# Graph attention on one core: the second attention's tiles written out in line, with a general pass behind them

## Chip, cores and metric

The kernel runs on one core of a Trainium2 chip. The metric is the device time of one execution in microseconds, the median of three runs. Within the core five engines work in parallel, each on its own instruction queue: TensorE (PE; its weight loads are PEld), VectorE (DVE), ScalarE (ACT), GpSimd (POOL) and SyncE (SP). They meet only at semaphores.

## What is computed

The reference is a stack of four layers over 6250 nodes of 256 numbers and 100,000 edges, sorted by destination: a cheap attention, a mixture of 6 experts, the graph attention that is changed here, and a mixture of 8 experts. Everything is float32. The third layer, cut to what matters (h is the normalised x times W, in 4 heads of 64):

```python
src = concatenate([edge_src, arange(n)]); dst = concatenate([edge_dst, arange(n)])
e = a_src[src] + a_dst[dst]              # 4 scores per edge
e = where(e > 0, e, 0.2 * e)
m = segment_max(e, dst)
ex = exp(e - m[dst])
denom = segment_sum(ex, dst)
alpha = ex / (denom[dst] + 1e-16)
out = segment_sum(alpha[:, :, None] * h[src], dst)
x = x + relu(out + bias)
```

How many edges end in a stretch of 128 nodes depends on the data: about 2048 (100,000 over 6250, times 128), a little more or less from tile to tile.

## The kernel before

The function `gnn_moe` runs the stages one after the other: `setup`, `project` and `experts` for the first layers, `project` "b0", `attention`, and again `project`, `experts` and `finish`.

**Tables.** Nodes are cut into 49 tiles of 128. During the first `project`, the class `EdgeRanges` finds for each tile the run of granules (32 edges each) that touches it. A *step* handles 17 chunks of 128 edges, 2176 edges or 68 granules (`SE`, `SEG`). The table `K.ET` holds for each tile its first edge, its number of steps n, and the number s0 of its first step. A tile whose run is longer than 68 granules has n = 2.

**One step of `attention`.** SP loads the source list `idx` and the destination list `dcol`, in three groups of 6, 6 and 5 chunks. POOL issues one indirect DMA for each chunk, which gathers 128 rows of 260 numbers (h and its score) into `G`. DVE compares the destinations with the ids of the tile (`one_hots`, into `OH`); PE transposes these one-hots (`turn`), ACT keeps them (`keep_turned`, into `OT`), and PE looks up the destination's part of the score (`destinations`, into `pAd`). DVE makes the scores (`scores`, four short instructions on `Z`), ACT takes the exponential (`exps`), DVE multiplies the gathered rows by it (`weigh`), and PE sums them by destination (`aggregate`, 17 matmuls that the trace shows as two records each, into `pAgg`). DVE adds that to `ACC` (`absorb`), and after a tile's last step divides, adds the bias and updates x (`finalize`).

**Loops.** Every engine runs loops over tiles, and within them over steps, with the number of steps read at run time from `K.ET`; POOL and ACT loop over all steps at once. What sets the order is each engine's written program and the semaphores. `G` has one buffer for each group of chunks, so a group's gathers of the next step wait until `aggregate` has read the last ones (`agg_done[j]`); other groups go on meanwhile, so the steps overlap.

Of the kernel before, what the change touches and what calls it, by code (L numbers as in the profile page):

```python
# [12 lines left out]
P = 128  # L13
# [30 lines left out]
GRAN = 32  # L44
# [47 lines left out]
def gnn_moe(nc, out, x, src, dst, L0_gnn_weight, L0_gnn_attn_l, L0_gnn_attn_r, L0_ffn_router_w1, L0_ffn_router_b1, L0_ffn_router_w2, L0_ffn_router_b2, L0_ffn_expert_w1, L0_ffn_expert_b1, L0_ffn_expert_w2, L0_ffn_expert_b2, L0_ffn_expert_w3, L0_ffn_expert_b3, L1_gnn_W, L1_gnn_att_src, L1_gnn_att_dst, L1_gnn_bias, L1_ffn_Wg, L1_ffn_bg, L1_ffn_W1, L1_ffn_b1, L1_ffn_W2, L1_ffn_b2):  # L92
    with ExitStack() as whole:
# [71 lines left out]
        K.ET = sb("edge_steps", [1, TILES, 3], I32)  # L165
        K.AD = sb("as_ad", [P, TILES, 8])
# [108 lines left out]
class EdgeRanges:  # L275
# [4 lines left out]
    def __init__(self, K, sb, sem):  # L280
# [9 lines left out]
        self.row = sb("row", [1, TILES, 2])  # L290
# [15 lines left out]
    def turn(self, gp):  # L306

        K = self.K
        gp.wait_ge(self.step, 13)
        gp.dma_start(K.RT[:, :], self.span[:, :]).then_inc(self.span_out, 16)  # L310
        gp.wait_ge(self.span_out, 16)
        gp.dma_start(self.row[0:1, :, :], K.RT.rearrange("(o t) k -> o t k", o=1)).then_inc(self.row_in, 16)
        gp.wait_ge(self.row_in, 16)
# [28 lines left out]
    def table(self, v):  # L342
# [8 lines left out]
        ch.mark(nc.vector.tensor_tensor(K.ET[0:1, :, 2], inc[0:1, :], row[0:1, :, 1], ALU.subtract))  # L351

# [966 lines left out]
def attention(K, bias_in):  # L1319
# [6 lines left out]
    J = range(len(CHUNKS))  # L1326
    with ExitStack() as stack:
# [4 lines left out]
        exs = sb("exs", [P, TILES, HEADS])  # L1332
        pm = sem("pm")
        gm_ready = sem("gm_ready")
        gm_all = sem("gm_all")
        self_z = sem("self_z")
        with nc.Block() as block:
            @block.vector
            def _(v):
                V = nc.vector  # L1340
                ch = Chain(v, pm)
                AS, ADs = K.AD[:, :, 0:4], K.AD[:, :, 4:8]
                ch.mark(V.tensor_reduce(gm[:, :].rearrange("p (h o) -> p h o", o=1),
                                        K.AD[:, 0:TILES - 1, 0:4].rearrange("p t h -> p h t"), AX.X, ALU.max))
                ch.link(V.tensor_scalar(gt[:, :], K.AD[:, TILES - 1, 0:4], K.vneg[:, 0:1], None, ALU.add))
                V.tensor_tensor(gm[:, :], gm[:, :], gt[:, :], ALU.max).then_inc(gm_ready, 1)
                v.wait_ge(gm_all, 1)
# [13 lines left out]
            @block.scalar  # L1361
            def _(act):
                act.wait_ge(self_z, 1)
                nc.scalar.activation(exs[:, :, :], exs[:, :, :], ACT.Exp)

        idx = [sb(f"idx{j}", [P, CHUNKS[j]], I32) for j in J]
        dcol = [sb(f"dcol{j}", [P, CHUNKS[j]]) for j in J]
        G = [sb(f"G{j}", [P, CHUNKS[j], DIM + 4]) for j in J]
        OH = [sb(f"OH{j}", [P, CHUNKS[j], P]) for j in J]
        OT = [sb(f"OT{j}", [P, CHUNKS[j], P]) for j in J]  # L1370
        Z = [sb(f"Z{j}", [P, CHUNKS[j], HEADS]) for j in J]
        own = sb("own", [P, DIM + 4])
        cur = sb("cur", [P, 8])
        ACC = sb("ACC", [P, DIM + 4])
        bias = sb("bias", [P, DIM])
        res = sb("res", [P, DIM])
        rec = sb("rec", [P, HEADS])
        pAd = [pb(f"pAd{j}", [P, 512]) for j in J]
        pAgg = pb("pAgg", [P, 512])


        pIds = pb("pIds", [P, 512])
        TI = pIds[:, 0:P]
        pEx = [pIds[:, P + j * 64:P + (j + 1) * 64] for j in J]
        pTr = [pb(f"pTr{h}", [P, 512]) for h in range(2)]

        bias_ld = sem("bias_ld")
        init = sem("init")
        src_in = [sem(f"src_in{j}") for j in J]
        dst_in = [sem(f"dst_in{j}") for j in J]  # L1390
        gathered = [sem(f"gathered{j}", software=True) for j in J]
        onehots = [sem(f"onehots{j}") for j in J]
        agg_done = [sem(f"agg_done{j}") for j in J]
        own_in = sem("own_in")
        own_used = sem("own_used")
        cur_ready = sem("cur_ready")
        ad_ready = sem("ad_ready")
        scored = [sem(f"scored{j}") for j in J]
        ex_ready = sem("ex_ready")
        msg_ready = sem("msg_ready")  # L1400
        acc_done = sem("acc_done")
        turned = sem("turned")
        ot_ready = sem("ot_ready")
        chain = sem("chain")
        passed = sem("passed")
        NJ = len(CHUNKS)
        lifts = (own_used, acc_done, ot_ready, *scored, *onehots, *agg_done)
        START, STEP, END = 2, 3 * NJ, 5

        def tile_steps(eng, t):  # L1410
            at = slice(t, t + 1) if isinstance(t, int) else bass.ds(t, 1)
            n = eng.value_load(K.ET[0:1, at, 1:2].rearrange("o a b -> o (a b)"), min_val=1, max_val=MAXSTEPS)
            s0 = eng.value_load(K.ET[0:1, at, 2:3].rearrange("o a b -> o (a b)"), min_val=0, max_val=TILES * MAXSTEPS)
            return n, s0

        with nc.Block() as block:
            @block.sync
            def _(sp):
                sp.dma_start(bias[:, :], bias_in.partition_broadcast(P)).then_inc(bias_ld, 16)
                with sp.Fori(0, TILES) as t:  # L1420
                    n, s0 = tile_steps(sp, t)
                    base = sp.value_load(K.ET[0:1, bass.ds(t, 1), 0:1].rearrange("o a b -> o (a b)"), min_val=0, max_val=EDGES - GRAN)
                    r0 = sp.snap(t * P)
                    freed(sp, own_used, t)
                    sp.dma_start(own[:, :], K.T1[bass.ds(r0, P), :]).then_inc(own_in, 16)
                    with sp.Fori(0, n) as g:
                        s = sp.snap(s0 + g)
                        e0 = nc.s_assert_within(sp.snap(base + g * SE), 0, EDGES, skip_runtime_bounds_check_because=
                                                "a step begins before its tile's last edge, and SE edges of padding follow the last")
                        at = [sp.snap(e0 + OFFS[j]) for j in J]  # L1430
                        for j in J:
                            ne = CHUNKS[j] * P
                            freed(sp, scored[j], s)
                            sp.dma_start(idx[j][:, :], K.SRCP[bass.ds(at[j], ne)].rearrange("(p c) -> p c", p=P)).then_inc(src_in[j], 16)
                            freed(sp, onehots[j], s)
                            sp.dma_start(dcol[j][:, :], K.DSTP[bass.ds(at[j], ne)].rearrange("(p c) -> p c", p=P)).then_inc(dst_in[j], 16)
# [3 lines left out]
            def _(gp):  # L1440
                lift(gp, lifts)
                n, s0 = tile_steps(gp, TILES - 1)
                with gp.Fori(0, gp.snap(s0 + n)) as s:
                    for j in J:
                        gp.wait_ge(src_in[j], s * 16 + 16)
                        freed(gp, agg_done[j], s)
                        gp.sem_inc(passed, 1)
                        for c in range(CHUNKS[j]):
                            gp.indirect_dma_start(G[j][:, c, :], None, K.T1,  # L1449
                                                  bass.IndirectOffsetOnAxis(ap=idx[j][:, c:c + 1], axis=0)).then_inc(gathered[j], 16)  # L1450

            @block.vector
            def _(v):
                V = nc.vector

                def one_hots(s, j):
                    c = CHUNKS[j]
                    v.wait_ge(dst_in[j], s * 16 + 16)
                    freed(v, agg_done[j], s)
                    V.tensor_tensor(OH[j][:, :, :], dcol[j][:, :].rearrange("p (c o) -> p c o", o=1).to_broadcast([P, c, P]),  # L1460
                                    TI.rearrange("p (o n) -> p o n", o=1).to_broadcast([P, c, P]),
                                    ALU.is_equal).then_inc(onehots[j], 1)

                def scores(ch, s, j):
                    c = CHUNKS[j]
                    v.wait_ge(gathered[j], s * (16 * c) + 16 * c)
                    v.wait_ge(ad_ready, s * NJ + j + 1)
# [224 lines left out]
```

## Time and profile before

| | |
|---|---|
| median of 3 runs | 3005.16 us (3003.9 to 3005.75) |
| the profiled execution's own time | 3002.53 us |
| span in its trace | 3000.9 us |
| second attention's gathers, first to last start | 921.20 to 1986.75 us |
| last update of x by the second attention | ends at 1998.46 us |
| mean granted TensorE clock | 0.822 |

The span is the time from the first to the last instruction of the profiled execution; 1.6 us of its own time lie outside it. Times within the trace count from the start of the span. Each row of a timeline has start, duration, engine, line and operation, output and inputs, and in square brackets how long the engine was idle before and what ended that.

### The profile page before, as it was taken

How to read it: one execution, taken by the hardware profiler on the slowest of the kernel's cores; microseconds unless marked ns; L12 is line 12 of the kernel's file. 1: busy time of each engine (PE TensorE's matmuls, PEld its weight loads, DVE VectorE, ACT ScalarE, POOL GpSimd, SP SyncE). 2: the span in 40 equal slices, each digit the busy share in tenths (PEclk: the TensorE clock that was granted, in tenths of full speed). 3: DMA queues.
4: the chain of work that ended last, by engine and by line, in shares of the span. 5: the costliest groups of instructions: out<-in, count | busy, mean ns of one | idle time of the engine just before them, and what ended most of it. 6: DMA issues, size and time to landing. Idle time of an engine off the chain costs nothing. (4 is left out here: it accounts for less than half of the span.)

```text
span 3000.9 us, 51618 instructions
## 1 busy us (share of the span) xinstructions
PE 2097.8 (70%) x12494; PEld 1844.3 (61%) x12495; DVE 1610.3 (54%) x4211; ACT 826.5 (28%) x2262; POOL 1437.8 (48%) x1457
## 2 busy tenths in 40 slices
PE   2533229898475787888878877866078998898970
PEld 2433227777354666666666666656078898888970
DVE  6365613222473556555555565556166655766555
ACT  1333302222141111111111111123044554545530
POOL 1267633333105777777777777736523322323220
PEclk8756569999796888888888888865589999999985
DMA  6212242222353444444444444422412221312207
GB/s 147 83 49 77 78 119 93 92 94 91 106 169 92 114 112 113 113 114 112 114 113 113 113 113 112 115 58 93 118 59 65 72 72 35 101 35 72 72 28 257
DMA packets 245332, 292.27 MB, mean 97 GB/s; under 512 B 102061, under 2 KB 199492, under 8 KB 245180
## 3 DMA queue, kind: packets, MB, share of 16 engines
q0 software_dynamic: 66224, 181.07, 20.9%
q1 hardware_dynamic: 165526, 97.08, 12.0%
q10 hardware_dynamic: 13544, 13.73, 1.4%
q14 instruction: 29, 0.24, 0.0%
q8 instruction: 9, 0.15, 0.0%
HBM read 213.94 MB, written 78.22 MB: 97 GB/s over the span
## 5 line engine op out<-in xcount | busy, mean ns | idle before, releaser
L1449 POOL DMA_INDIRECT at_G<-h_as,at_idx x850 | 806.7, 949 | 269.2 <-issue 256.4
L1600 PE MATMUL at_pAgg<-at_G,at_OH 128*128 128x260 f32 x1700 | 542.1, 484 | 158.6 <-DVE at_ACC L1498 95.7
L1600 PEld LDWEIGHTS at_pAgg<-at_G,at_OH 128*128 128x128 f32 x1700 | 404.5, 245 | 260.4 <-DVE at_G L1480 179.2
L1063 POOL DMA_INDIRECT expert_out<-e_ob,e_to x212 | 205.1, 968 | 743.5 <-DVE e_ob L1294 711.2
L1480 DVE TENSOR_TENSOR at_G<-at_G,at_pIds 128x1536 f32<-128x1536 f32 x150 | 249.8, 1665 | 151.4 <-ACT at_pIds L1565 151.4
L1267 DVE TENSOR_TENSOR e_hT_low<-e_full,e_hT_high 128x256 fp32r<-128x256 f32 x432 | 226.4, 531 | 156.9 <-ACT e_hT_high L1214 155.9
L1137 PE MATMUL e_pH<-e_xT_high,e_WA_high 128*128 128x256 f32 x864 | 257.2, 298 | 75.3 <-DVE e_xT_low L1229 68.1
L1558 ACT ACTIVATE at_OT<-at_pTr 128x384 f32<-128x384 f32 (+1 forms) x300 | 125.8, 470 | 656.8 <-PE at_pTr L1585 656.5
L1213 ACT ACTIVATE e_full<-e_pH,e_BA 128x256 f32<-128x256 f32 x432 | 219.0, 507 | 206.8 <-PE e_pH L1139 136.8
L1138 PE MATMUL e_pH<-e_xT_low,e_WA_high 128*128 128x256 f32 x864 | 249.3, 289 | 0.0
L1139 PE MATMUL e_pH<-e_xT_high,e_WA_low 128*128 128x256 f32 x864 | 249.1, 288 | 0.0
L1137 PE MATMUL e_pO<-e_WL_high,e_hT_high 128*128 128x256 f32 x864 | 245.1, 284 | 0.5 <-DVE e_ob L1294 0.5
L1138 PE MATMUL e_pO<-e_WL_low,e_hT_high 128*128 128x256 f32 x864 | 240.7, 279 | 0.0
L1139 PE MATMUL e_pO<-e_WL_high,e_hT_low 128*128 128x256 f32 x864 | 240.4, 278 | 0.0
L1593 PEld LDWEIGHTS at_pAd<-at_cur,at_OT 128*128 128x128 f32 x1700 | 208.7, 201 | 43.6 <-ACT at_OT L1558 43.6
L1593 PE MATMUL at_pAd<-at_cur,at_OT 128*128 128x8 f32 x1700 | 212.4, 261 | 31.7 <-ACT at_OT L1558 31.7
L1137 PEld LDWEIGHTS e_pH<-e_xT_high,e_WA_high 128*128 128x128 f32 x864 | 172.7, 200 | 83.6 <-issue 72.0
L1214 ACT ACTIVATE e_hT_high<-e_pH,e_BA 128x256 fp32r<-128x256 f32 x432 | 220.7, 511 | 0.0
L1138 PEld LDWEIGHTS e_pH<-e_xT_low,e_WA_high 128*128 128x128 f32 x864 | 172.5, 200 | 0.0
L1139 PEld LDWEIGHTS e_pH<-e_xT_high,e_WA_low 128*128 128x128 f32 x864 | 171.5, 199 | 0.0
L1137 PEld LDWEIGHTS e_pO<-e_WL_high,e_hT_high 128*128 128x128 f32 x864 | 162.4, 188 | 0.7 <-DVE e_ob L1294 0.7
L1138 PEld LDWEIGHTS e_pO<-e_WL_low,e_hT_high 128*128 128x128 f32 x864 | 162.3, 188 | 0.0
(294 smaller groups left out, 3680.2 us busy)
## 6 DMA issues: line engine op xcount, KB each, us to landing
e_xs<-slot_rows SPq DMA_DIRECT2D x106, 257.0 KB
at_G<-h_as,at_idx POOLq DMA_INDIRECT x850, 2.8
b_rows<-expert_out SPq DMA_DIRECT2D x14, 896.0 KB
f_rows<-expert_out ACTq DMA_DIRECT2D x14, 896.0 KB, 7.7
e_rawA<-in_L_ffn_W_dram SPq DMA_DIRECT2D x8, 1024.0 KB, 5.0
e_rawL<-in_L_ffn_W_dram SPq DMA_DIRECT2D x8, 1024.0 KB
xt_ar<-a_og SPq DMA_DIRECT2D x7, 910.0 KB, 4.5
h_as<-b_og SPq DMA_DIRECT2D x7, 910.0 KB, 4.2
```

The lines of the kernel that those rows point to most:

```text
L1063: gp.indirect_dma_start(K.YS, bass.IndirectOffsetOnAxis(ap=to[b][:, s:s + 1], axis=0), ob[b][:, s, :], None).then_inc(sent[b], 16)
L1137: nc.tensor.matmul(out, left[0], right[0], start=start, stop=False)
L1138: nc.tensor.matmul(out, left[0], right[1], start=False, stop=False)
L1139: return nc.tensor.matmul(out, left[1], right[0], start=False, stop=stop)
L1213: nc.scalar.activation(full[u % 4][:, :], pH[u % 4][:, 0:MT], func, bias=at)
L1214: nc.scalar.activation(dst[b][0][:, c, :], pH[u % 4][:, 0:MT], func, bias=at).then_inc(h_ready, 1)
L1267: V.tensor_tensor(hT[b][1][:, u, :], full[u % 4][:, :], hT[b][0][:, u, :], ALU.subtract).then_inc(l_ready, 1)
L1449: gp.indirect_dma_start(G[j][:, c, :], None, K.T1, bass.IndirectOffsetOnAxis(ap=idx[j][:, c:c + 1], axis=0)).then_inc(gathered[j], 16)
L1480: V.tensor_tensor(rows, rows, ex, ALU.mult).then_inc(msg_ready, 1)
L1558: nc.scalar.activation(OT[j][:, a:z, :].rearrange("n c p -> n (c p)"), pTr[h][:, 0:(z - a) * P], ACT.Copy).then_inc(ot_ready, 1)
L1593: last = nc.tensor.matmul(pAd[j][:, 8 * c:8 * c + 8], OT[j][:, c, :], cur[:, :], start=True, stop=True)
L1600: last = nc.tensor.matmul(pAgg[:, 0:DIM + 4], OH[j][:, c, :], G[j][:, c, :], start=(j == 0 and c == 0), stop=(j == NJ - 1 and c == CHUNKS[ ...
```

## The change

There are now two passes in `attention`.

The **first pass** has no loops: SP, POOL, DVE, ACT and PE have the 49 tiles written out, one step for each. SP loads each tile's lists in one piece each, one tile ahead. `idx`, `dcol`, `own`, `OH`, `pAd` and `pAgg` have two buffers; `G`, `OT` and `Z` still have one for each group. DVE subtracts the tile's first id from the destinations (`localize`) and makes the one-hots of tile t + 1 before and between the scores of tile t. PE transposes them there too, and does all of a tile's lookups at its beginning. `finalize(t - 1)` starts the sum from the node's own row and takes `pAgg` in.

The **general pass** stands behind it and has loops over tiles and steps. In it, everything has one buffer. SP starts a step's loads when the step before is in `ACC` (`absorbed`), and DVE and POOL wait for all three of them (`loaded`); ACT begins the exponentials when all three groups are scored, DVE the weighing when all three exponentials are there, and PE the sums when all three groups are weighed.

Two new values in the tables join them. `K.FAST` is 1 when no tile has more than one step, else 0; `K.GEN` is 49 - 49 * `K.FAST` and is the number of tiles that the general pass runs over. The first pass always runs; its quotient and its bias are multiplied by `K.FAST`, so that with 0 it adds nothing to x. The row of step counts is for that loaded into all 128 partitions.

```diff
+        K.FAST = sb("one_step_each", [P, 1])
+        K.GEN = sb("general_tiles", [1, 1], I32)
...
+        ch.link(nc.vector.tensor_reduce(self.most[:, :], row[:, :, 1], AX.X, ALU.max))
+        ch.link(nc.vector.tensor_scalar(K.FAST[:, :], self.most[:, :], 1.5, None, ALU.is_lt))
+        ch.mark(nc.vector.tensor_scalar(K.GEN[:, :], K.FAST[0:1, :], -float(TILES), float(TILES), ALU.mult, ALU.add))
...
+                ch.mark(V.tensor_scalar(bias[:, :], GB[:, :], K.FAST[:, 0:1], None, ALU.mult))
...
+                for t in range(TILES):
+                    b, n = t % 2, 16 * (t // 2 + 1)
+                    e0 = sp.value_load(K.ET[0:1, t:t + 1, 0:1].rearrange("o a b -> o (a b)"), min_val=0, max_val=EDGES - GRAN)
+                    after(sp, scored, NJ * (t - 1))
+                    sp.dma_start(idx[b][:, :], K.SRCP[bass.ds(e0, SE)].rearrange("(p c) -> p c", p=P)).then_inc(idx_in[b], 16)
+                    after(sp, localized, t - 1)
+                    sp.dma_start(dcol[b][:, :], K.DSTP[bass.ds(e0, SE)].rearrange("(p c) -> p c", p=P)).then_inc(dst_in[b], 16)
+                    after(sp, own_used, t - 1)
+                    sp.dma_start(own[b][:, :], K.T1[t * P:(t + 1) * P, :]).then_inc(own_in[b], 16)
...
+                for t in range(TILES):
+                    b = t % 2
+                    gp.wait_ge(idx_in[b], 16 * (t // 2 + 1))
                     for j in J:
-                        gp.wait_ge(src_in[j], s * 16 + 16)
-                        freed(gp, agg_done[j], s)
-                        gp.sem_inc(passed, 1)
+                        after(gp, agg_done, NJ * (t - 1) + j + 1)
...
+                def finalize(t):
+
+                    b = t % 2
+                    v.wait_ge(own_in[b], 16 * (t // 2 + 1))
+                    V.tensor_tensor(ACC[:, 0:DIM].rearrange("p (h k) -> p h k", h=HEADS),
+                                    own[b][:, 0:DIM].rearrange("p (h k) -> p h k", h=HEADS),
+                                    exp_self[:, t, :].rearrange("p (h o) -> p h o", o=1).to_broadcast([P, HEADS, CH]), ALU.mult).then_inc(own_used, 1)
+                    ch.link(V.tensor_copy(ACC[:, DIM:DIM + 4], exp_self[:, t, :]))
+                    v.wait_ge(own_used, t + 1)
+                    v.wait_ge(agg_done, NJ * (t + 1))
+                    V.tensor_tensor(ACC[:, :], ACC[:, :], pAgg[b][:, 0:DIM + 4], ALU.add).then_inc(acc_read, 1)
+                    v.wait_ge(acc_read, t + 1)
...
+                    ch.link(V.tensor_scalar(rec[:, :], rec[:, :], K.FAST[:, 0:1], None, ALU.mult))
...
+                localize(0)
+                for j in J:
+                    one_hots(0, j)
+                for t in range(TILES):
+                    more = t + 1 < TILES
+                    if more:
+                        localize(t + 1)
+                        one_hots(t + 1, 0)
+                        one_hots(t + 1, 1)
+                    scores(t, 0)
+                    weigh(t, 0)
+                    if t:
+                        finalize(t - 1)
+                    if more:
+                        one_hots(t + 1, 2)
+                    scores(t, 1)
+                    weigh(t, 1)
+                    scores(t, 2)
+                    weigh(t, 2)
+                finalize(TILES - 1)
...
+                for j in J:
+                    turn(0, j)
+                for t in range(TILES):
+                    for j in J:
+                        destinations(t, j)
+                    for j in J:
+                        if t + 1 < TILES:
+                            turn(t + 1, j)
+                        aggregate(t, j)
...
+                m = general_tiles(sp)
+                with sp.If(m > 0):
+                    with sp.Fori(0, m) as t:
+                        n, s0 = general_steps(sp, t)
+                        first = sp.value_load(K.ET[0:1, bass.ds(t, 1), 0:1].rearrange("o a b -> o (a b)"), min_val=0, max_val=EDGES - GRAN)
+                        r0 = sp.snap(t * P)
+                        with sp.Fori(0, n) as g:
+                            s = sp.snap(s0 + g)
+                            e0 = nc.s_assert_within(sp.snap(first + g * SE), 0, EDGES, skip_runtime_bounds_check_because=
+                                                    "a step begins before its tile's last edge, and SE edges of padding follow the last")
+                            freed(sp, absorbed, s)
+                            sp.dma_start(idx[0][:, :], K.SRCP[bass.ds(e0, SE)].rearrange("(p c) -> p c", p=P)).then_inc(loaded, 16)
+                            sp.dma_start(dcol[0][:, :], K.DSTP[bass.ds(e0, SE)].rearrange("(p c) -> p c", p=P)).then_inc(loaded, 16)
+                            sp.dma_start(own[0][:, :], K.T1[bass.ds(r0, P), :]).then_inc(loaded, 16)
...
+                            gp.wait_ge(loaded, s * 48 + 48)
+                            gp.sem_inc(passed, 1)
+                            for j in J:
+                                for c in range(CHUNKS[j]):
+                                    gp.indirect_dma_start(G[j][:, c, :], None, K.T1,
+                                                          bass.IndirectOffsetOnAxis(ap=idx[0][:, FIRST[j] + c:FIRST[j] + c + 1], axis=0)).then_inc(got[j], 16)
...
+                    for j in J:
+                        c = CHUNKS[j]
+                        v.wait_ge(got[j], s * (16 * c) + 16 * c)
+                        v.wait_ge(looked_up, s + 1)
+                        ad = pAd[0][:, 8 * FIRST[j]:8 * (FIRST[j] + c)].rearrange("p (c k) -> p c k", k=8)
+                        ch.link(V.tensor_tensor(Z[j][:, :, :], G[j][:, :, DIM:DIM + 4], ad[:, :, 0:4], ALU.add))
+                        ch.link(V.scalar_tensor_tensor(Z[j][:, :, :], Z[j][:, :, :], 0.2, Z[j][:, :, :], ALU.mult, ALU.max))
+                        ch.link(V.tensor_tensor(Z[j][:, :, :], Z[j][:, :, :], ad[:, :, 4:8], ALU.subtract))
+                        V.tensor_scalar(Z[j][:, :, :], Z[j][:, :, :], 0.0, None, ALU.min).then_inc(rated, 1)
+                    for j in J:
+                        c = CHUNKS[j]
+                        v.wait_ge(weights_made, s * NJ + NJ)
+                        rows = G[j][:, :, 0:DIM].rearrange("p c (h k) -> p c h k", h=HEADS)
+                        ex = pEx[j].rearrange("p (c h o) -> p c h o", h=HEADS, o=1).to_broadcast([P, c, HEADS, CH])
+                        V.tensor_tensor(rows, rows, ex, ALU.mult).then_inc(weighed, 1)
+                    v.wait_ge(summed, s + 1)
+                    ch.mark(V.tensor_tensor(ACC[:, :], ACC[:, :], pAgg[0][:, 0:DIM + 4], ALU.add))
+                    ch.settle()
+                    v.sem_inc(absorbed, 1)
+
...
+                            for j in J:
+                                act.wait_ge(rated, s * NJ + NJ)
+                                nc.scalar.activation(G[j][:, :, DIM:DIM + 4], Z[j][:, :, :], ACT.Exp)
+                                nc.scalar.activation(pEx[j].rearrange("p (c h) -> p c h", h=HEADS), Z[j][:, :, :],
+                                                     ACT.Exp).then_inc(weights_made, 1)
...
+                            pe.wait_ge(weighed, s * NJ + NJ)
+                            for j in J:
+                                for c in range(CHUNKS[j]):
+                                    last = nc.tensor.matmul(pAgg[0][:, 0:DIM + 4], OH[0][j][:, c, :], G[j][:, c, :],
+                                                            start=(j == 0 and c == 0), stop=(j == NJ - 1 and c == CHUNKS[j] - 1))
+                            last.then_inc(summed, 1)
```

On SP, the issue order changes as follows. These rows are the loop body of before: `g_edge_steps` is the table read into registers, and three pairs of small loads make a step.

```order
L1425 DMA at_own<-h_as 128x260
L1426 UNCONDITIONAL_BRANCH
L1426 ISA
L1434 ISA
L1434 DMA at_idx<-src_padded 128x6
L1436 DMA at_dcol<-dst_padded 128x6
L1434 ISA
L1434 DMA at_idx<-src_padded 128x6
L1436 DMA at_dcol<-dst_padded 128x6
L1434 ISA
L1434 DMA at_idx<-src_padded 128x5
L1436 DMA at_dcol<-dst_padded 128x5
```

And this is the general pass's loop on SP in the changed kernel, from the last of its three table loads on:

```order
L1629 TENSOR_LOAD g_edge_steps
L1629 ISA x2
L1631 UNCONDITIONAL_BRANCH
L1631 ISA
L1636 ISA
L1636 DMA at_idx<-src_padded 128x17
L1637 DMA at_dcol<-dst_padded 128x17
L1638 ISA
L1638 DMA at_own<-h_as 128x260
L1631 REGISTER_ALU
L1631 COMPARE_AND_BRANCH
```

Three loads take the place of seven, the node's own rows last, and the whole list of a step comes in one piece. The first pass, ahead of it, has the same three kinds of load written out 49 times.

On DVE, before, the last group of a tile's step and the start of a further step of the same tile; `at_pIds` holds the tile's ids and the exponentials:

```order
L1480 TENSOR_TENSOR at_G<-at_G,at_pIds 128x5x256
L1531 COMPARE_AND_BRANCH
L1532 UNCONDITIONAL_BRANCH
L1532 ISA
L70 REGISTER_ALU
L1460 TENSOR_TENSOR at_OH<-at_dcol,at_pIds 128x768 x2
```

And in the general pass of the changed kernel, from the last group's last score to the update of `ACC` and on into the division:

```order
L1679 TENSOR_SCALAR at_Z<-at_Z 128x20
L1682 ISA
L1685 TENSOR_TENSOR at_G<-at_G,at_pExs 128x6x256 x2
L1685 TENSOR_TENSOR at_G<-at_G,at_pExs 128x5x256
L1687 TENSOR_TENSOR at_ACC<-at_ACC,at_pAgg 128x260
L85 REGISTER_ALU
L1707 REGISTER_ALU
L1707 COMPARE_AND_BRANCH
L1713 TENSOR_SCALAR at_rec<-at_ACC 128x4
```

The three multiplications stand together behind the last score, and the update of `ACC` stands directly behind them, where before other groups' and steps' work lay between.

## Rows read from the trace of the kernel before

**Rows 1.** The page's first line: span and instructions.

```profile
span 3000.9 us, 51618 instructions
```

**Rows 2.** Groups, 921 to 1997 us: count, busy us, mean ns, idle before.

```profile
L1449 POOL DMA_INDIRECT at_G<-h_as,at_idx x850 | 806.7, 949 | 269.2 <-issue 256.4 <-DMA at_idx<-src_padded 12.2 <-PE at_pAgg L1600 0.6
...
L1498 DVE TENSOR_TENSOR at_ACC<-at_ACC,at_pAgg 128x260 f32<-128x260 f32 x50 | 20.9, 418 | 3.1 <-PE at_pAgg L1600 3.1
...
L1524 DVE TENSOR_TENSOR at_ACC<-at_own,at_exs 128x256 f32<-128x256 f32 x49 | 20.4, 417 | 0.0
...
L1515 DVE TENSOR_SCALAR at_pIds<-at_pIds 128x128 f32<-128x128 f32 x48 | 14.4, 299 | 29.7 <-issue 29.7
```

**Rows 3.** Windows view: busy us of each engine, granted clock, DMA.

```profile
core 0: us, PE busy (x) PEld busy (x) DVE busy (x) ACT busy (x) POOL busy (x), PEclk, DMA share, GB/s
921.00:1997.00 1076.00, 863.15 (x4250) 711.52 (x4250) 620.17 (x1386) 165.63 (x600) 806.73 (x850) 0.83 0.43 112
```

**Rows 4.** Timeline of DVE, 1630 to 1662 us.

```profile
1630.40 0.30 DVE L1515 TENSOR_SCALAR at_pIds<-at_pIds 128x128 f32<-128x128 f32 x1 [0.63 <-issue]
...
1651.19 1.81 DVE L1460 TENSOR_TENSOR at_OH<-at_dcol,at_pIds 128x768 f32<-128x768 f32 x2
```

**Rows 5.** Timeline: DVE frees the own rows, SP's next load follows.

```profile
1513.42 0.42 DVE L1524 TENSOR_TENSOR at_ACC<-at_own,at_exs 128x256 f32<-128x256 f32 x1
...
1514.02 0.33 SPq L1425 DMA_DIRECT2D at_own<-h_as  x1
```

**Rows 6.** Timeline: the attention's first loads and gather.

```profile
914.94 0.36 SPq L1419 DMA_DIRECT2D at_bias<-in_L_gnn_bias_dram  x1
...
917.64 0.36 SPq L1425 DMA_DIRECT2D at_own<-h_as  x1
918.41 0.34 SPq L1434 DMA_DIRECT2D at_idx<-src_padded  x1
918.84 0.38 SPq L1436 DMA_DIRECT2D at_dcol<-dst_padded  x1
...
920.55 1.85 DVE L1460 TENSOR_TENSOR at_OH<-at_dcol,at_pIds 128x768 f32<-128x768 f32 x2 [0.98 <-DMA at_dcol<-dst_padded]
...
921.20 1.19 POOL L1449 DMA_INDIRECT at_G<-h_as,at_idx  x1 [9.48 <-DMA at_idx<-src_padded]
```

**Rows 7.** DMA issues, 921 to 1997 us: KB each, us to landing.

```profile
at_own<-h_as SPq DMA_DIRECT2D x48, 130.0 KB, 2.1
```

**Rows 8.** Timeline: the attention's last group, to its last update.

```profile
1986.75 0.95 POOL L1449 DMA_INDIRECT at_G<-h_as,at_idx  x1 [0.30 <-issue]
...
1990.45 0.17 DVE L1469 TENSOR_TENSOR at_Z<-at_G,at_pAd 128x20 f32<-128x20 f32 x1 [0.79 <-DMA at_G<-h_as,at_idx]
...
1991.29 0.22 ACT L1564 ACTIVATE at_G<-at_Z 128x20 f32<-128x20 f32 x1 [3.41 <-DVE at_Z L1473]
...
1991.62 1.49 DVE L1480 TENSOR_TENSOR at_G<-at_G,at_pIds 128x1280 f32<-128x1280 f32 x1 [0.36 <-ACT at_pIds L1565]
1996.24 0.42 DVE L1498 TENSOR_TENSOR at_ACC<-at_ACC,at_pAgg 128x260 f32<-128x260 f32 x1 [3.14 <-PE at_pAgg L1600]
...
1998.04 0.42 DVE L1509 SCALAR_TENSOR_TENSOR g_x<-at_res,g_x 128x256 f32<-128x256 f32 x1
```

**Rows 9.** Timeline of PE: sums of two groups, and lookups.

```profile
933.57 5.00 PE L1600 MATMUL at_pAgg<-at_G,at_OH 128*128 128x260 f32 x12 [3.99 <-DVE at_G L1480]
...
989.68 2.46 PE L1600 MATMUL at_pAgg<-at_G,at_OH 128*128 128x260 f32 x10 [0.28 <-DVE at_G L1480]
...
994.32 2.74 PE L1593 MATMUL at_pAd<-at_cur,at_OT 128*128 128x8 f32 x24
```

**Rows 10.** Windows view of PE: length, busy us, granted clock, DMA.

```profile
935.50:937.50 2.00, 2.00 (x6) 0.50 0.66 178
937.50:939.00 1.50, 1.50 (x9) 0.88 0.32 89
...
945.50:948.00 2.50, 1.58 (x8) 1.00 0.46 109
```

More of the change, by code:

```diff
@@ L1326, in attention @@
     J = range(len(CHUNKS))
+    NJ = len(CHUNKS)
+    CH_ALL = sum(CHUNKS)
+    FIRST = [sum(CHUNKS[:j]) for j in J]
+    HALVES = [(j, a, z) for j in J for a, z in ((0, 3), (3, CHUNKS[j]))]
     with ExitStack() as stack:
@@ L1332, in attention @@
         exs = sb("exs", [P, TILES, HEADS])
+        pIds = pb("pIds", [P, 512])
+        TI = pIds[:, 0:P]
+        exp_self = pIds[:, P:P + TILES * HEADS].rearrange("p (t h) -> p t h", h=HEADS)
+        bias = sb("bias", [P, DIM])
+        GB = sb("general_bias", [P, DIM])
         pm = sem("pm")
@@ L1368, in attention @@
+        own = [sb(f"own{b}", [P, DIM + 4]) for b in range(2)]
         G = [sb(f"G{j}", [P, CHUNKS[j], DIM + 4]) for j in J]
-        OH = [sb(f"OH{j}", [P, CHUNKS[j], P]) for j in J]
+        OH = [[sb(f"OH{b}_{j}", [P, CHUNKS[j], P]) for j in J] for b in range(2)]
         OT = [sb(f"OT{j}", [P, CHUNKS[j], P]) for j in J]
         Z = [sb(f"Z{j}", [P, CHUNKS[j], HEADS]) for j in J]
-        own = sb("own", [P, DIM + 4])
-        cur = sb("cur", [P, 8])
         ACC = sb("ACC", [P, DIM + 4])
-        bias = sb("bias", [P, DIM])
@@ L1376, in attention @@
         res = sb("res", [P, DIM])
         rec = sb("rec", [P, HEADS])
[L1378 to L1384, printed above, removed]
+        pAd = [pb(f"pAd{b}", [P, 512]) for b in range(2)]
+        pAgg = [pb(f"pAgg{b}", [P, 512]) for b in range(2)]
+        pExs = pb("pExs", [P, 512])
+        pEx = [pExs[:, FIRST[j] * HEADS:(FIRST[j] + CHUNKS[j]) * HEADS] for j in J]
@@ L1402, in attention, with after @@
-        turned = sem("turned")
-        ot_ready = sem("ot_ready")
+        agg_done = sem("agg_done")
+        acc_read = sem("acc_read")
         chain = sem("chain")
[L1405 to L1414, printed above, removed]
+        def after(eng, s, n):
+            if n > 0:
+                eng.wait_ge(s, n)
@@ L1418, in _ @@
             def _(sp):
[L1419 to L1436, printed above, removed]
@@ L1552, in _, with keep_turned @@
+                finalize(TILES - 1)
             @block.scalar
             def _(act):
-                def keep_turned(s, j):
-                    for h, (a, z) in enumerate(((0, 3), (3, CHUNKS[j]))):
-                        act.wait_ge(turned, s * (2 * NJ) + (2 * j + h + 1))
+                def keep_turned(t, j):
+                    for h in range(2):
+                        k = t * len(HALVES) + 2 * j + h
+                        _, a, z = HALVES[2 * j + h]
+                        act.wait_ge(turned, k + 1)
@@ new lines, in attention, with general_steps @@
+        looked_up = sem("looked_up")
+        rated = sem("rated")
+        weights_made = sem("weights_made")
+        weighed = sem("weighed")
+        summed = sem("summed")
+        absorbed = sem("absorbed")
+        order = sem("order")
+        passed = sem("passed")
+        base = sb("base", [P, 1])
+        def general_steps(eng, t):
+            at = bass.ds(t, 1)
+            n = eng.value_load(K.ET[0:1, at, 1:2].rearrange("o a b -> o (a b)"), min_val=1, max_val=MAXSTEPS)
+            s0 = eng.value_load(K.ET[0:1, at, 2:3].rearrange("o a b -> o (a b)"), min_val=0, max_val=TILES * MAXSTEPS)
+            return n, s0
```

301 lines of the change are left out of this document (169 added, 132 removed).

## The prediction

> **What bounds the kernel now.** I read the page first for the span, 3000.9 us [rows 1], and took as the stretch of this change the time in which its gathers run, 921 to 1997 us. The view of groups says who works there: POOL issues 850 gathers, and the idle time before them is nearly all "issue", waiting for nothing; for PE's sums it waited 0.6 us in all [rows 2]. The first gather starts at 921.20 [rows 6] and the last at 1986.75 [rows 8], so one gather takes (1986.75 - 921.20) / 849 = 1.255 us, without a pause at the turns of the loops. The windows view bears this out from the other side: PE is busy for 863 of 1076 us and DVE for 620 [rows 3]. So POOL's queue sets the end of this stage: 17 gathers make 21.3 us for a step, and everything else of a step hides beside them.
>
> 850 gathers of 17 to a step are 50 steps, and there are 49 tiles. The reader is to see the same in two other counts: `ACC` takes `pAgg` in 50 times (L1498), but the node's own row starts it 49 times (L1524) [rows 2]. The timeline shows where: the tile that starts at 1630.40 with new ids (L1515) gets a second pair of one-hots at 1651.19 with no new ids ahead of them [rows 4]. One tile, about two thirds into the stretch, has more than 2176 edges in its run. That it is one in 49 doesn't matter for the kernel before, which pays one step of 21.3 us for it.
>
> **The change part by part.** *The switch.* `K.FAST` asks for the largest count of steps over all tiles. That is 2, so `K.FAST` is 0 and `K.GEN` is 49: the first pass runs in full with its result multiplied by 0, and then the general pass does all 49 tiles again, in 50 steps. The title's words could be read as a pass for that one tile alone; the arithmetic has nothing between 0 and 49.
>
> *The first pass.* POOL issues 49 x 17 = 833 gathers, one step fewer than before. Is it still POOL that sets its pace? I count one tile from its first gather. The last gather of the tile before was issued 1.255 us ahead of that, and its scores begin 3.70 us after its issue (1986.75 to 1990.45), at 2.4; score, exponential and weighing of 5 chunks take 2.7 us (1990.45 to 1993.11) [rows 8]; its sums 2.5 us and then 34 records of lookups at 24 in 2.74, 3.9 us [rows 9]. At 11.5 this tile's first group can be scored and weighed, 3.0 us, and its 12 sums take 12 x 0.246 = 3.0: `G`'s first group is free at 17.5, before POOL comes back at 21.3. DVE gets one subtraction of 17 columns and one product of 4 for a copy and the ids' update; it is busy for 620 / 50 = 12.4 us of a step [rows 3]. So I take no new wait: -21.3 us for the step saved. The worst end has PE at its low clock throughout: lookups and sums then take 4.2 + 6.6 + 5.0 us in place of 9.4 (0.417 in place of 0.246 us a record [rows 9], lookups in the same ratio), 6.4 more, and `G` is free at 23.9: +2.6 x 49 = +127.
>
> *Loop turns.* What the writing out removes is the time at the turns: on DVE 29.7 us of "issue" ahead of L1515 in 48 turns [rows 2]. It lies beside POOL's gathers, so its price here is nothing; if DVE set the pace it would be worth up to 29.7 us. The Trainium skill, "Runtime: NRT & Kernel Launch", section Instruction fetch mechanics, says that a taken branch to code outside the window fetched makes the engine wait, and that kernels for this reason prefer full unrolling; DVE's row agrees, POOL's doesn't show it, and by that rule alone the sum would be lower by those 29.7 us.
>
> *The general pass.* Here nothing overlaps from step to step: SP's loads wait for `absorbed`, which is the step's last act. One step, from one update of `ACC` to the next:
> - SP wakes 0.2 us after DVE's end (1513.84 to 1514.02) [rows 5]. Its second load starts 0.43 us behind the first; the own rows, third, I put 0.6 behind that (between 0.43 and the 0.77 seen between own and list) [rows 6]. With 0.35 for that issue and 2.1 us to landing [rows 7], all is in after 3.65 us. POOL is slower to start than DVE: 2.79 us after its list's issue, DVE 1.71 after its own [rows 6]. I take half that difference: 4.2 us to the first gather. Bounds 3.2 (landing together, no delay) and 5.2 (the whole delay, slower issues).
> - 16 gathers of 1.255 us and then 3.70 us to the last group's score: 23.8 us. One-hots, transposes, lookups and the other groups' scores hide under these, and so do the loop turns and table loads of all engines.
> - The last group's four score operations: 0.84 us (1990.45 to 1991.29). Then three pairs of exponentials, now together: from one pair's start to the weighing behind it are 0.33 us (1991.29 to 1991.62), three times 1.0 us [rows 8].
> - Three weighings: 1.49 us for 1280 columns [rows 8], so 1.79 for 1536: 5.1 us.
> - 34 records of sums without a pause. PE has by then been idle for over 10 us, and starts at a granted clock of 0.50, that is 1.2 GHz, as it did at 933.57 [rows 9, 10]: 12 records in 5.00 us, 0.417 each; at the full clock, 2.4 GHz, 10 take 2.46, 0.246 each [rows 9]. There the clock rose about 4.4 us after the start [rows 10]. So 10.5 records at the low clock and 23.5 at the high one: 10.2 us. To this come start and drain: `ACC` began at 1996.24, 3.13 us after a weighing whose 10 records take 2.46, so 0.7 us [rows 8, 9]. Sum 10.9; bounds 9.1 (all high) and 14.9 (all low).
> - The update of `ACC` and its settling: 0.45 us [rows 8].
>
> Together 4.2 + 23.8 + 0.84 + 1.0 + 5.1 + 10.9 + 0.45 = 46.3 us, and 50 of them 2315 us. The division and bias of a tile lie under the next loads. Once, there is the entry, 2.7 us from the phase's start to its first table-dependent load (914.94 to 917.64) [rows 6], and the last division, 1.8 us (1996.66 to 1998.46) [rows 8]: 5 us with the change of phase.
>
> *Small edits.* Three more DVE operations in the tables, one for the bias, and a wider row load, once each: 2 us, nothing if hidden.
>
> The sum: 3000.9 - 21.3 + 2315 + 5 + 2 = 5301.6 us of span. The profiled run's own time was 1.6 us above its span, and the median 2.6 us above that time (3005.16 against 3002.53): 5306 us. Its own range: 50 x (3.2 + 23.8 + 0.8 + 0.9 + 5.0 + 9.1 + 0.4) = 2160 and 50 x (5.2 + 23.9 + 0.9 + 1.2 + 5.2 + 14.9 + 0.5) = 2590 are the ends of the pass, 5151 and 5581 of the time. The low end needs several terms at their least at once.
>
> **The rivals.**
> - *The sums stay at the low clock*, as the first 12 did [rows 9]. 34 x 0.417 + 0.7 = 14.9 us, 4.0 more a step: 5306 + 200 = 5506. For it: PE works little in this pass, two short bursts in 46 us. Against: a burst of the length needed did raise the clock within it [rows 10]. Chance 0.12.
> - *The first pass becomes bound by PE*. `G`'s first group is freed only when all lookups of a tile and two sets of transposes are behind it. At 2.5 us a tile: 5306 + 122 = 5428. For it: PE has the least room, 863 of 1076 us [rows 3]. Against: the count above. Chance 0.08.
> - *The other side, faster: the general pass doesn't run.* If the largest count were 1, `K.GEN` would be 0, and only the saved step and the small edits would remain: 3005.2 - 21.3 + 2 + 1 = 2987 us. It decides at one place, the maximum over the row of counts; that 50 steps ran for 49 tiles [rows 2] speaks against it as plainly as a trace can. Chance 0.02.
> - *The change does what its title may be read to say*, a general pass for the one tile alone: two steps more, 3005 - 21 + 92 + 6 = 3082 us. `K.GEN` can't be 1. Chance 0.01.
>
> **How the numbers follow.** The likeliest case has 0.77. The range takes it in with both of the slower rivals, and leaves the two short ones and the ends out: 5170 to 5530. A measurement of this kernel tells about 0.2% from no change. Faster by more 0.02, within it 0.01, slower 0.97.
>
> **What would show it.** After the change the trace should have 833 gathers of the first pass at a pace of 1.255 us from about 921 to 1966 us, then 850 in bursts of 17, each burst starting 46 us after the last; 50 updates of `ACC` in the second pass and none of x with a value in the first. PE's sums should stand alone, with the clock rising in their midst. The prediction is wrong if there is only one set of gathers; if the bursts are closer than 43 us, a wait that I put in series overlaps; if they are farther apart than 52, something between `absorbed` and the first gather, or the clock, costs more than any row here shows.

## The result, and the profile after

The changed kernel takes 5455.55 us (median of 4 runs, 5448.08 to 5457.27), the kernel before beside it 3004.53 us: 1.8154 times as long, 95% interval 1.8123 to 1.8186. The forecast was 5306 us in a range of 5170 to 5530. The likeliest case happened: the general pass ran over all 49 tiles. But the first pass, priced at 21.3 us less than the loops that it replaced, became slower than they were.

The span of the profiled execution is 5446.2 us. The page's groups have both sets of gathers (count, busy us, mean ns, idle before and what ended most of it):

```profile
L1654 POOL DMA_INDIRECT at_G<-h_as,at_idx x850 | 803.5, 945 | 1409.8 <-DMA at_own<-h_as 1166.1
L1448 POOL DMA_INDIRECT at_G<-h_as,at_idx x833 | 787.8, 946 | 509.0 <-PE at_pAgg L1584 269.4
```

Against [rows 2], one POOL line has become two, 833 and 850 gathers. The cost of one is unchanged, 946 ns. What changed is what it waits for: in the first pass 269.4 us for PE's sums, where it was 0.6, and in the general pass 1166.1 us for the loads that open a step, 23.3 us a step, most of it the chain of work that has to end before these loads are issued.

The view of the tile `G` (`at_G`), changed kernel, places them in time (count: min/median/max ns, first and last start):

```profile
L1654 POOL DMA_INDIRECT at_G<-h_as,at_idx x850: 940/946/962, 2233.2 to 4426.4; - x170
L1448 POOL DMA_INDIRECT at_G<-h_as,at_idx x833: 940/946/1190, 923.2 to 2213.1; - x167
```

The first pass issues one gather in (2213.1 - 923.2) / 832 = 1.550 us, 26.4 us a tile in place of 21.3. A windows view of the changed kernel, a stretch of each pass, has the answer to [rows 3]:

```profile
core 0: us, PE busy (x) PEld busy (x) DVE busy (x) ACT busy (x) POOL busy (x), PEclk, DMA share, GB/s
1500.00:1800.00 300.00, 214.71 (x952) 178.13 (x951) 139.85 (x313) 36.15 (x136) 181.53 (x192) 0.74 0.34 91
3000.00:3444.00 444.00, 222.17 (x854) 186.14 (x853) 124.58 (x280) 35.12 (x120) 160.85 (x171) 0.61 0.21 54
```

No engine is full in either: PE is busy for 72% in the first pass and 50% in the general one, at a mean granted clock of 0.74 and 0.61. Work is waiting in turns, not for room.

**One step of the general pass**, timeline of the changed kernel (start, duration, engine and line):

```profile
3006.41 0.94 POOL L1654 DMA_INDIRECT at_G<-h_as,at_idx  x1 [0.30 <-issue]
3009.18 0.18 DVE L1676 TENSOR_TENSOR at_Z<-at_G,at_pAd 128x20 f32<-128x20 f32 x1 [5.41 <-DMA at_G<-h_as,at_idx]
...
3010.02 0.22 ACT L1737 ACTIVATE at_G<-at_Z 128x24 f32<-128x24 f32 x1 [16.07 <-DVE at_Z L1679]
...
3010.79 4.82 DVE L1685 TENSOR_TENSOR at_G<-at_G,at_pExs 128x1536 f32<-128x1536 f32 x3 [0.81 <-ACT at_pExs L1738]
3015.67 10.48 PE L1765 MATMUL at_pAgg<-at_G,at_OH 128*128 128x260 f32 x34 [14.16 <-DVE at_G L1685]
3026.19 0.42 DVE L1687 TENSOR_TENSOR at_ACC<-at_ACC,at_pAgg 128x260 f32<-128x260 f32 x1 [10.58 <-PE at_pAgg L1765]
3026.90 0.33 SPq L1636 DMA_DIRECT2D at_idx<-src_padded  x1
...
3030.70 0.95 POOL L1654 DMA_INDIRECT at_G<-h_as,at_idx  x1 [23.35 <-DMA at_own<-h_as]
```

Read from top to bottom, each row is released by the one above: last gather, score, exponentials, three weighings in one row, 34 records of sums, `ACC`, loads, next gather. Between the gathers at 3006.41 and 3030.70 POOL issues nothing.

**Where the first pass goes round**: timelines of the changed kernel's DVE, PE, POOL and ACT, one after the other:

```profile
1606.58 0.18 DVE L1479 TENSOR_SCALAR at_Z<-at_Z 128x24 f32<-128x24 f32 x1
1609.51 1.75 DVE L1486 TENSOR_TENSOR at_G<-at_G,at_pExs 128x1536 f32<-128x1536 f32 x1 [2.75 <-ACT at_pExs L1545]
...
1602.23 5.57 PE L1584 MATMUL at_pAgg<-at_G,at_OH 128*128 128x260 f32 x12 [2.56 <-DVE at_G L1486]
1607.59 1.12 PE L1565 MATMUL at_pTr<-g_ident,at_OH 128*128 128x128 f32 x6
1611.32 4.58 PE L1584 MATMUL at_pAgg<-at_G,at_OH 128*128 128x260 f32 x12 [2.62 <-DVE at_G L1486]
...
1621.09 3.86 PE L1575 MATMUL at_pAd<-at_adm,at_OT 128*128 128x8 f32 x34
...
1628.48 4.66 PE L1584 MATMUL at_pAgg<-at_G,at_OH 128*128 128x260 f32 x12 [2.56 <-DVE at_G L1486]
...
1608.57 0.94 POOL L1448 DMA_INDIRECT at_G<-h_as,at_idx  x1 [5.26 <-PE at_pAgg L1584]
...
1608.41 0.87 ACT L1538 ACTIVATE at_OT<-at_pTr 128x384 f32<-128x384 f32 x2 [8.03 <-PE at_pTr L1565]
1609.17 0.22 ACT L1544 ACTIVATE at_G<-at_Z 128x24 f32<-128x24 f32 x1
```

Group 1 is scored at 1606.76, but its exponential starts at 1609.17: ACT keeps the next tile's transposes first (L1538), and on PE these stand behind the sums of group 0 (1602.23 to 1607.8). Only then come exponential, weighing and, at 1611.32, the sums of group 1, for which PE has waited 2.62 us. Group 2 repeats this behind group 1, with a wait of 2.35 us on PE. Behind the sums of group 2 stand the next tile's lookups (1621.09) and the first transposes of the tile after it, then its group 0 with 2.56 us, and at 1628.48 the ring is round: 26.25 us after 1602.23, without having passed POOL once.

### The profile page after: what moved, and what is told of

The parts are those of the page before. It is cut to its first block and busy times, and to the rows that moved or that the text cites. A ratio compares the mean times of both kernels' runs of the same rounds, so it can differ in the third digit from the quotient of the medians.

```text
span 5446.2 us, 64206 instructions
## 1 busy us (share of the span) xinstructions
PE 3266.6 (60%) x16659; PEld 2825.7 (52%) x16660; DVE 2221.0 (41%) x5589; ACT 992.2 (18%) x2850; POOL 2223.8 (41%) x2290
## 5 line engine op out<-in xcount | busy, mean ns | idle before, releaser
L1654 POOL DMA_INDIRECT at_G<-h_as,at_idx x850 | 803.5, 945 | 1409.8 <-DMA at_own<-h_as 1166.1
L1448 POOL DMA_INDIRECT at_G<-h_as,at_idx x833 | 787.8, 946 | 509.0 <-PE at_pAgg L1584 269.4
L1765 PE MATMUL at_pAgg<-at_G,at_OH 128*128 128x260 f32 x1700 | 521.8, 481 | 726.2 <-DVE at_G L1685 726.2
L1765 PEld LDWEIGHTS at_pAgg<-at_G,at_OH 128*128 128x128 f32 x1700 | 414.4, 247 | 817.9 <-DVE at_G L1685 730.9
L1584 PE MATMUL at_pAgg<-at_G,at_OH 128*128 128x260 f32 x1666 | 606.4, 535 | 365.2 <-DVE at_G L1486 365.2
L1584 PEld LDWEIGHTS at_pAgg<-at_G,at_OH 128*128 128x128 f32 x1666 | 442.4, 275 | 505.9 <-DVE at_G L1486 407.7
L1753 PE MATMUL at_pTr<-g_ident,at_OH 128*128 128x128 f32 x850 | 214.1, 429 | 374.4 <-DVE at_OH L1669 374.4
L1486 DVE TENSOR_TENSOR at_G<-at_G,at_pExs 128x1536 f32<-128x1536 f32 x147 | 244.8, 1665 | 393.1 <-ACT at_pExs L1545 393.1
L1759 PEld LDWEIGHTS at_pAd<-at_adm,at_OT 128*128 128x128 f32 x1700 | 353.9, 322 | 47.7 <-issue 47.7
L1753 PEld LDWEIGHTS at_pTr<-g_ident,at_OH 128*128 128x128 f32 x850 | 146.7, 214 | 442.4 <-issue 394.5
L1759 PE MATMUL at_pAd<-at_adm,at_OT 128*128 x1700 | 358.4, 354 | 28.1 <-ACT at_OT L1733 28.1
L1676 DVE TENSOR_TENSOR at_Z<-at_G,at_pAd 128x24 f32<-128x24 f32 x150 | 26.7, 178 | 846.4 <-PE at_pAd L1759 529.6
L1733 ACT ACTIVATE at_OT<-at_pTr 128x384 f32<-128x384 f32 (+1 forms) x300 | 138.4, 472 | 1227.0 <-PE at_pTr L1753 1212.0
L1538 ACT ACTIVATE at_OT<-at_pTr 128x384 f32<-128x384 f32 (+1 forms) x294 | 128.4, 471 | 1125.3 <-PE at_pTr L1565 1118.2
L1685 DVE TENSOR_TENSOR at_G<-at_G,at_pExs 128x1536 f32<-128x1536 f32 x150 | 240.8, 1661 | 40.4 <-ACT at_pExs L1738 40.4
```

Source lines behind the costliest of these rows:

```text
L1448: gp.indirect_dma_start(G[j][:, c, :], None, K.T1, bass.IndirectOffsetOnAxis(ap=idx[b][:, FIRST[j] + c:FIRST[j] + c + 1], axis=0)).then_in ...
L1486: V.tensor_tensor(rows, rows, ex, ALU.mult).then_inc(msg_ready, 1)
L1584: last = nc.tensor.matmul(pAgg[t % 2][:, 0:DIM + 4], OH[t % 2][j][:, c, :], G[j][:, c, :], start=(j == 0 and c == 0), stop=(j == NJ - 1 an ...
L1654: gp.indirect_dma_start(G[j][:, c, :], None, K.T1, bass.IndirectOffsetOnAxis(ap=idx[0][:, FIRST[j] + c:FIRST[j] + c + 1], axis=0)).then_in ...
L1685: V.tensor_tensor(rows, rows, ex, ALU.mult).then_inc(weighed, 1)
L1753: last = nc.tensor.transpose(pTr[k % 2][:, (c - a) * P:(c - a + 1) * P], OH[0][j][:, c, :], K.ident[:, :])
```

## Experiments

Twelve runs follow: eight different kernels, three of them run again on a second chip, and the changed kernel itself once more. All edits are to the changed kernel unless said; each time is beside runs of the kernel before on the same chip.

**1. The first pass alone** (`e1`). One tile's second step, with the last 26 of its 2184 edges, is left out in this and every run called "alone" (the expectation says 8, which is 2184 less the 2176 of a step and overlooks that the tile's first step begins with 18 edges of its neighbour).

```diff
-        ch.link(nc.vector.tensor_scalar(K.FAST[:, :], self.most[:, :], 1.5, None, ALU.is_lt))
+        ch.link(nc.vector.tensor_scalar(K.FAST[:, :], self.most[:, :], 2.5, None, ALU.is_lt))
```

> The bound in K.FAST is 2.5 in place of 1.5, so that the two-step tile counts as one, K.GEN is 0 and only the first pass does the work; the last 8 of the 34th tile's edges are left out. Theory (the two passes are paid one after the other, and the first pass alone is slower than the loops of before): 5455 less the general pass, 2224 us, gives about 3232 us, some 228 above before. Rival (the first pass is only slow because its result is thrown away or the general pass's code disturbs it): about 2987 us, as predicted for the case without a general pass.

3232.55 us, 1.0777 times the kernel before (1.0759 to 1.0796). So the first pass by itself is slower than the loops, by 7.8%, with one step less to do. POOL waits 270.4 us for PE's sums in it, as in the changed kernel.

**2. Exponentials first on ACT** (`e2`, the first pass alone).

```diff
                 for t in range(TILES):
                     for j in J:
+                        exps(t, j)
                         if t + 1 < TILES:
                             keep_turned(t + 1, j)
-                        exps(t, j)
```

> The first pass alone, with ACT taking the exponentials of tile t's group before it keeps the transposes of tile t + 1's. Theory (exponentials stand on ACT behind the next tile's transposes, these on PE behind the sums of the group before, so that the three groups of a tile go in a ring): the ring is broken, POOL's gathers set the pace again, 21.3 to 22.5 us a tile in place of 26.4, and the time falls to 2985 to 3045 us. Rival (PE's work itself is too much, with all lookups in one piece at a low clock): above 3180 us, hardly changed.

2996.63 us, 0.9989 (0.998 to 0.9999): 236 us less than with the other order. This moves nothing but two instructions on ACT in each group, and the work of PE is the same. The ring stands; that PE's work was too much falls. The gathers now start 1060.8 us apart from first to last, where they took 1289.9. The view of `G` in this kernel, gathers and POOL's wait for the sums (us, times):

```profile
L1448 POOL DMA_INDIRECT at_G<-h_as,at_idx x833: 942/946/1190, 922.4 to 1983.2; - x167
...
  POOL at_G L1448: 20.5, 23
```

**3. Transposes ahead on PE** (`e3`, the first pass alone, ACT as in the change).

```diff
-                    for j in J:
-                        if t + 1 < TILES:
-                            turn(t + 1, j)
-                        aggregate(t, j)
+                    more = t + 1 < TILES
+                    if more:
+                        turn(t + 1, 0)
+                        turn(t + 1, 1)
+                    aggregate(t, 0)
+                    if more:
+                        turn(t + 1, 2)
+                    aggregate(t, 1)
+                    aggregate(t, 2)
```

> The first pass alone, ACT as it was, but PE transposes groups 0 and 1 of the next tile before the sums of group 0, and group 2 before the sums of group 1. Theory of the ring: the same ring is broken on PE's side for one of its two turns, the other stays; 22 to 24 us a tile, 3020 to 3120 us. Rival (PE's work is too much): above 3180 us, since PE does the same work.

2995.69 us, 0.9993 (0.9981 to 1.0005). I had expected only part of the gain, 3020 to 3120 us; the whole of it came. A lead of one group is enough: the transposes of group 1 now stand before the sums of group 0, and those of group 2 before the sums of group 1, so neither turn of the ring is left. POOL's waits for PE are 13.6 us.

**4. Both passes, exponentials first** (`e4`): experiment 2's edit in the changed kernel.

> The changed kernel with both passes, with ACT's exponentials first. Theory of the ring: the first pass gives back what the first pass alone does, about 190 to 245 us, the general pass nothing: 5210 to 5265 us. Rival (the passes affect each other, or the clock is used up): less than 150 us back.

5212.86 us, 1.7379 (1.735 to 1.7408): 243 us less than the changed kernel, which ran on another chip, or about 233 us by the two ratios. The general pass's updates of `ACC` still run over 2173 us (2036.4 to 4209.5; 2174 us in the changed kernel). The passes' costs simply add.

**5. The general pass by groups** (`e5`, again as `e9`).

```diff
-                    for j in J:
-                        c = CHUNKS[j]
-                        v.wait_ge(weights_made, s * NJ + NJ)
+                        v.wait_ge(weights_made, s * NJ + (j + 1))
...
-                                act.wait_ge(rated, s * NJ + NJ)
+                                act.wait_ge(rated, s * NJ + (j + 1))
...
-                            pe.wait_ge(weighed, s * NJ + NJ)
                             for j in J:
+                                pe.wait_ge(weighed, s * NJ + (j + 1))
```

> The changed kernel with both passes; in the general pass exponentials, weighing and sums of a group wait for that group alone. Theory (a step's terms are in series, and only what stands behind the last landing counts): behind the last score one exponential pair, one weighing and 10 records remain, so 0.45 + 3.4 + 6.3 to 8.0 us a step go, 510 to 590 in all: 4865 to 4945 us. Rival (the sums are on PE's low clock when they are cut up, or DVE's queue puts the groups in series anyway): less than 400 us back, above 5050.

This run and the next two fell on a chip on which the kernel before takes 3530.77 us, so their times can't be set beside the others. `e5` took 5645.35 us, 1.5983 times that. In its general pass a first group's scores began at 3340.05, 4.1 us after the step's last gather was issued and 17.8 us after the last gather of their own group (3322.24), though PE's lookups, the other thing they wait for, had ended at 3330.3. The three were run again on another chip, with the changed kernel itself (`e8`) as the control.

> The changed kernel as it is, as a control beside the next three. Theory: 1.815 times the kernel before if this chip's transfers land as on the first chip. Rival (a chip on which gathers land late, as in the last three runs, where the kernel before took 3531 us): a smaller ratio, near 1.75, since both kernels get longer by the same hundreds of us or the series by less.

> The general pass by groups, again, now beside the changed kernel itself on the same chip. Theory (only what stands behind the last landing counts): 510 to 590 us below the changed kernel. Rival: less than 400 us below it, since in the trace of the last run the weighing of the last group ended 3.9 us before the sums did, so that PE's low clock takes part of the gain back.

`e8` took 5456.69 us (1.8162, 1.8132 to 1.8193), `e9` 4889.12 us (1.6284, 1.6257 to 1.6311): 568 us or 11.4 us a step less. The end of a step in the timeline of `e9`:

```profile
3010.84 0.17 DVE L1676 TENSOR_TENSOR at_Z<-at_G,at_pAd 128x20 f32<-128x20 f32 x1 [3.33 <-DMA at_G<-h_as,at_idx]
...
3016.05 0.42 DVE L1685 TENSOR_TENSOR at_ACC<-at_ACC,at_pAgg 128x260 f32<-128x260 f32 x1 [2.55 <-PE at_pAgg L1763]
```

From the last group's score to `ACC` are 5.2 us, where the changed kernel has 17.0 (3009.18 to 3026.19).

**6. Eighteen chunks** (`e6`, again as `e10`): experiment 2's edit, and steps of 2304 edges, so that every tile has one step and the general pass none. Nothing is left out.

```diff
-CHUNKS = (6, 6, 5)
+CHUNKS = (6, 6, 6)
```

> The changed kernel with ACT's exponentials first and 18 chunks in a step in place of 17 (groups of 6, 6, 6), so that no tile has two steps and the general pass has no tile. Theory (POOL's gathers set the pace once the ring is broken): 49 x 18 = 882 gathers of 1.255 us, 32 more than before, +40 us: 3035 to 3065 us. Rival (one more chunk fills PE): above 3100 us.

> 18 chunks, ACT's exponentials first, again. Theory (POOL's gathers set the pace): 32 gathers more than before, +40 us: 1.010 to 1.020 times the kernel before. Rival (one more chunk fills PE): above 1.03.

On the chip with 3530.77 us it took 3664.9 (1.0375, 1.0347 to 1.0403); on the other 3055.93 us (1.0175, 1.0158 to 1.0192), 52 us above the kernel before. 32 gathers more explain 40 of these. A guarantee of one step for every tile costs more gathers than the one second step it saves.

**7. The kernel before with eighteen chunks** (`e7`, again as `e11`), the same one-line edit there.

> The kernel before with 18 chunks in a step. Theory (the loops cost nothing beside POOL's gathers): the same 882 gathers, 3004 + 40 = 3044 us, within 10 us of the changed kernel with 18 chunks. Rival (the loops' turns are on the path and the written-out pass saves them): slower than the changed kernel with 18 chunks by 20 us or more.

> The kernel before with 18 chunks, again. Theory (the loops cost nothing beside POOL's gathers): within 10 us of the changed kernel with 18 chunks. Rival (the loops' turns are on the path): slower than that by 20 us or more. A third way, after the last runs: the changed kernel with 18 chunks is the slower one, because it depends more on when the gathers land.

3508.31 us on the one chip (0.9938, 0.9917 to 0.9959) and 3054.4 us on the other (1.0172, 1.0155 to 1.0189), 1.5 us from the written-out kernel with the same chunks. The two differ in orders and buffers too, so this compares the whole forms: the written-out one waits longer for PE's sums (19.5 us against 4.3). But little was to be had from the turns. In the kernel before POOL waits 2.7 us for source lists behind its first gather (12.2 in all [rows 2], 9.5 of them before it) and 0.6 for sums. The rival that the loops' turns are on the path, worth 20 us or more, falls. On the chip with late gathers the loops are the faster by 157 us.

**8. Both orders** (`e12`, the first pass alone, experiments 2 and 3 together).

> The first pass alone with both edits, exponentials first on ACT and transposes ahead on PE. Theory (what is left of the saved step of 21.3 us goes into POOL's waits for PE's sums, 20.5 us with ACT's edit and 13.6 us with PE's, and these come from the order): waits below 10 us, and 10 to 18 us below the kernel before. Rival (they come from PE's work at its low clock, which either order has): waits of 10 us or more and at most 8 us below the kernel before.

2988.26 us, 0.9966 (0.9955 to 0.9976), 11.5 us below the kernel before. POOL's wait for PE's sums in this kernel (us in all, times, longest):

```profile
POOL at_G L1448 <- PE at_pAgg L1584: 7.3, 15, 1.2
```

So most of what the waits had left of the saved step was order too. This is the best that the first pass gave, and it leaves the 26 edges out; no written-out version with all edges beat the kernel before. (The loops with eighteen chunks did so by 0.6%, on the chip with 3530.77 us alone.)

## Why the prediction was right, and what it had wrong

*The switch* was read rightly, from three counts: 850 gathers, 50 updates and 49 starts of `ACC` [rows 2]. It decides nearly all of the time. The forecast had the phase of the general pass at 2315 + 5 us; from the first pass's last update of x (end at 2225.8) to its own last (4448.9) it took 2223.

*The terms of a step.* 44.4 us (2272.4 to 4446.2 in 49 steps) in place of 46.3. First gather after `ACC`: 4.1 us (3026.61 to 3030.70) against 4.2. Last gather to last score: 2.8 us against 3.70, the largest error, 0.9 us. The row that I had read in [rows 8] is an odd one: in the kernel before DVE waited for a group's gathers 44 times, and in the 43 others the score began 2.82 to 2.96 us after the group's last gather was issued, in the same stage of 112 GB/s [rows 3]. I had taken one late landing for the rule. Such late ones, of 3.4 us or more, are seen now and then in the full stage of other runs too (6 of 47 waits in `e2`, 5 of 48 in `e3`, 3 of 45 in `e12`) and in none of 100 waits of the general pass; whether the traffic makes them late was not tried. Exponentials 0.8 against 1.0, weighings 4.9 against 5.1. From the weighing to `ACC` it is 10.6 us against 10.9, in which two errors offset each other. The 34 records took 10.48 us against 10.2, with the granted clock at 0.50 still from 3020.80 to 3021.20 and at 1.00 from 3021.40, so it rose some 5.6 us after their start and not 4.4. And `ACC` followed the last record by 0.04 us, not by 0.7, which in [rows 8] was time in which PE still worked at the group before (22 records without a pause from 1989.72 to 1996.21). The rival of a clock that stays low did not occur. The pass took 97 us less than forecast.

*The step that failed* is "So I take no new wait: -21.3 us for the step saved". From the first gather (923.2) to the last update of x the first pass took 1302.6 us, where the loops took 1077.3 (921.20 to 1998.46): +225 instead of -21, 247 us off. I had followed one tile's first group through PE and found it free at 17.5 us. What I left out was ACT's queue, in which group j's exponential stands behind transposes that PE makes only after group j - 1's sums, so that groups 1 and 2 go one after the other. The pace of 1.255 us a gather, which the prediction named as what the trace should have, was 1.550. The rival "the first pass becomes bound by PE" had the place (`G` freed late) and half the price, 2.5 us a tile against 5.0; its cause was wrong, as experiment 2 shows: the order of two instructions on another engine gives back 236 us with PE's work unchanged. The "worst end" of my own count, 2.6 us a tile, came from one engine's load and was too low as well.

The two errors, +247 and -97, nearly make the whole of 5455.55 - 5306 = 149.6 us. That the number fell into the range is in part luck: with the first pass's error alone it would have been about 5553 us, above the upper end of 5530. That end had been drawn for a slow clock and for PE, not for the ring, and the general pass came out 97 us short.

*Loop turns.* They were priced at nothing, since they lie beside POOL's gathers, and experiments 6 and 7 bear that out: the two forms differ by 1.5 us. The Trainium skill ("Runtime: NRT & Kernel Launch", Instruction fetch mechanics) says that kernels prefer full unrolling where possible, because a taken branch can make an engine wait for its instructions. Here that preference gave nothing: POOL sets the pace and shows no such wait, and DVE's turns, 29.7 us in all, lie beside it.

*The low-probability cases* (no general pass, or one for the single tile) didn't occur. Experiment 1 shows that the first of them would not have been faster at all but 7.8% slower, where I had given 2987 us.

## What to carry to other kernels

Before a loop is written out, find the engine that sets the pace; when it doesn't stop at the loop's turns, nothing is to be had there. When work of the next tile is put ahead in several queues at once, follow one group through all of them as a ring, each engine's queue with what stands before it: one instruction put ahead on an otherwise idle engine (ACT, 12% busy) can put groups in series. A fast path with a switch over all tiles pays its fall-back in full if the data has one exception, so count the exceptions in the trace first.

## What the runs showed of the hardware

Two things were not expected. One chip ran the unchanged kernel in 3530.77 us where the others gave 2999 to 3005, and there the order of two kernels with eighteen chunks turned from a difference of 1.5 us to one of 157 us. Scores that waited for gathers began late there (17.8 us after the group's last gather, experiment 5); why was not settled. And the time from a group's last gather to the score that waits for it was nearly the same at both levels of traffic: 2.71 to 2.90 us in 100 waits of the general pass (54 GB/s), 2.82 to 2.96 in 43 of 44 waits of the full stage before (112 GB/s), with the 3.70 of [rows 8] the one exception. Only the full stages had such late ones.
